# Slot tables of routing: two of each group's seven blocks multiplied by VectorE instead of ScalarE

## What is computed

```
gate_scores = einsum('bsd,ed->bse', x, Wg) + bg
topk_scores, topk_idx = top_k(gate_scores, 2)
topk_probs = softmax(topk_scores, axis=-1)
combine = sum(topk_probs[..., None] * one_hot(topk_idx, 8), axis=-2)
for e in range(8):
    h = relu(einsum('bsd,hd->bsh', x, W1[e]) + b1[e])
    y = einsum('bsh,dh->bsd', h, W2[e]) + b2[e]
    out = out + combine[..., e:e + 1] * y
```

## Time and profile before

| | us |
|---|---|
| median of three runs | 2040.22 |
| lowest and highest of them | 2038.3, 2041.55 |
| the profiled execution, its own time | 2043.48 |
| its span in the profile | 2041.8 |

### The profile page before, as it was taken

One profiled execution on the slowest core, in us unless ns is written; L12 is line 12 of the kernel. 1 busy time (PEld: TensorE's weight loads), 2 busy tenths in 40 slices (PEclk: granted clock), 3 DMA queues, 4 the chain that ended last, 5 costly groups with the idle time before them and its releaser, 6 DMA issues. The chain is left out here.

```text
span 2041.8 us, 50410 instructions
## 1 busy us (share of the span) xinstructions
PE 1662.7 (81%) x15119; PEld 1287.6 (63%) x15119; DVE 1579.0 (77%) x3370; ACT 1379.6 (68%) x3988; POOL 1247.3 (61%) x1226
## 2 busy tenths in 40 slices
PE   5777668888888788898886666562799999999998
PEld 3455557666666577777764344342677777777776
DVE  8899859898888899989998989887355555555554
ACT  7565458788887778888878878575455555555554
POOL 4357757777777777777777777650344444444443
PEclk7899979999999999999999999855899999999999
DMA  6122355555554544444433346461344444444442
GB/s 223 44 70 80 110 167 157 158 157 159 153 160 151 158 139 124 124 124 121 122 106 101 102 154 185 130 206 26 78 72 73 73 74 71 72 74 71 74 71 43
DMA packets 197501, 232.75 MB, mean 114 GB/s; under 512 B 89207, under 2 KB 154657, under 8 KB 197123
## 3 DMA queue, kind: packets, MB, share of 16 engines
q0 software_dynamic: 62816, 134.68, 25.8%
q1 hardware_dynamic: 128070, 88.47, 15.4%
q10 hardware_dynamic: 6364, 6.40, 0.9%
HBM read 172.28 MB, written 44.36 MB: 106 GB/s over the span
## 5 line engine op out<-in xcount | busy, mean ns | idle before, releaser
L1011 POOL DMA_INDIRECT misc<-z_d,consts x814 | 784.6, 964 | 265.0 <-issue 160.6
L1261 DVE SCALAR_TENSOR_TENSOR acc<-ps,consts,acc 128x512 f32 x814 | 609.2, 748 | 79.3 <-PE ps L1363 60.7
L1034 ACT ACTIVATE misc<-misc 128x256 f16<-128x256 f16 x872 | 391.2, 498 | 74.5 <-DVE misc L1128 69.0
L1891 ACT ACTIVATE misc<-ps,misc 128x128 f32<-128x128 f32 x840 | 240.2, 368 | 276.1 <-PE ps L1851 166.9
L1361 PE MATMUL ps<-misc 128*128 128x256 f16 x1088 | 298.1, 274 | 110.7 <-ACT misc L1034 35.6
L1939 POOL DMA_INDIRECT out<-misc,pos x105 | 166.4, 1585 | 295.5 <-ACT misc L1960 244.7
L1849 PE MATMUL ps<-acc,big 128*128 128x128 f16 x1680 | 328.3, 220 | 14.9 <-DMA acc<-acc 10.0
L1851 PE MATMUL ps<-acc,big 128*128 128x128 f16 x1680 | 330.0, 220 | 0.0
L1850 PE MATMUL ps<-acc,big 128*128 128x128 f16 x1680 | 327.9, 220 | 0.0
L1870 PE MATMUL ps<-big,rec 128*128 x840 | 320.5, 382 | 0.1
L1363 PE MATMUL ps<-misc 128*128 128x256 f16 x1088 | 298.8, 275 | 0.0
(11 more groups left out here) (348 smaller groups left out, 3657.8 us busy)
## 6 DMA issues: line engine op xcount, KB each, us to landing
big<-in_w2T SPq DMA_DIRECT2D x60, 256.0 KB, 2.7
misc<-z_d,consts POOLq DMA_INDIRECT x814
big<-xT_d SPq DMA_DIRECT2D x98, 128.0 KB
big<-in_w1T SPq DMA_DIRECT2D x32, 256.0 KB, 2.8
tok_d<-misc SPq DMA_DIRECT2D x50, 132.0 KB, 1.8
xT_d<-misc SPq DMA_DIRECT2D x49, 128.0 KB
z_d<-misc SPq DMA_DIRECT2D x49, 128.0 KB, 1.7
acc<-in_x SPq DMA_DIRECT2D x6, 896.0 KB
```

Source lines behind the costliest of these rows:

```text
L1011: e.indirect_dma_start(out=rows[n % RB], out_offset=None, in_=c.z_d, in_offset=bass.IndirectOffsetOnAxis(ap=idx[u][:, k:k + 1], axis=0)).t ...
L1034: e.activation(hot[n % HG][:, half, :], same[n % OG], ACT.Copy, scale=near[n // UG % 3][:, t % UG, 1 + half:2 + half]).then_inc(s_hot, 1)
L1261: e.scalar_tensor_tensor(out=rows_of, in0=out_ps[tile % BG], scalar=c.gain, in1=rows_of, op0=ALU.mult, op1=ALU.add).then_inc(s_add, 1)
L1891: l = e.activation(hidden[:, m, :], h_ps[u][:, m, :], ACT.Relu, bias=b1x[u][:, m:m + 1])
```

## The change

VectorE multiplies the last two blocks of each group (`NA` = 5 and 6) in two instructions of 2 x 105 elements, one for each of the two choices. Here `near_no` is a second tensor input, one value repeated over 105 elements. ScalarE does the blocks 0 to 4 alone. The new instructions stand in `hots`, between `hot_tile` and `hot_row`, and wait for `hot_tile` and for `s_used`; `hot_row` no longer stands directly behind that wait. `group(g)` waits for a new semaphore `s_rest` as well.

```diff
+    s_rest = S("near_rest")
+    NA = 5
+    of_blocks = lambda a, lo, hi: a.rearrange("p (k n) m -> p k n m", k=TOP)[:, :, lo:hi, :]
...
                 e.tensor_tensor(hot_tile[g % 2], row_no[:, 0:MT, :], tiled(both16[0][:, g, :], MT), ALU.is_equal).then_inc(s_tiles, 1)
+                e.wait_ge(s_tiles, g + 1)
                 if g >= 2:
                     e.wait_ge(s_used, g - 1)
+                for k in range(TOP):
+                    l = e.tensor_tensor(of_blocks(pieces[g % 2][:, :, 0, :], NA, GB)[:, k],
+                                        of_blocks(hot_tile[g % 2].rearrange("p m c -> p c m"), NA, GB)[:, k],
+                                        near_no[:, g * GB + NA:g * GB + GB].rearrange("p (n a) -> p n a", a=1).to_broadcast([P, GB - NA, MT]),
+                                        ALU.mult)
+                l.then_inc(s_rest, 1)
                 e.tensor_tensor(hot_row[g % 2], row_no, tiled(both16[1][:, g, :], P), ALU.is_equal).then_inc(s_rows, 1)
 
             def group(g):
                 e.wait_ge(s_near, g + 1)
+                e.wait_ge(s_rest, g + 1)
                 e.tensor_scalar(pieces[g % 2][:, :, 1, :], pieces[g % 2][:, :, 0, :], 0.0, float(g), ALU.is_gt,
                                 ALU.mult).then_inc(s_group, 1)
...
-                halves = lambda a, n: a.rearrange("p (k n) m -> p k n m", k=TOP)[:, :, n, :]
-                for n in range(GB):
+                halves = lambda a, n: of_blocks(a, n, n + 1)[:, :, 0, :]
+                for n in range(NA):
                     l = e.activation(halves(pieces[g % 2][:, :, 0, :], n),
```

## The result

| | before | changed |
|---|---|---|
| median, us (14 runs each) | 2041.11 | 2045.01 |
| lowest to highest | 2038.3 to 2043.81 | 2042.93 to 2049.44 |
| the profiled execution, its own time | 2043.48 | 2042.93 |
| its span | 2041.8 | 2041.2 |
| the block: first `hot_tile` to first gather | 35.32 | 39.71 |

The ratio of the times is 1.0022 with a 95% interval of 1.0015 to 1.003: slower by 3.1 to 6.1 us, 4.5 in the middle; the two medians stand 3.90 apart. 2044.8 had been predicted. The two profiled executions seem to say the opposite, since the changed one is 0.6 us shorter. The next view, busy time by stretch (PE, PEld, DVE, ACT, POOL, clock, DMA share, GB/s), divides each span into what lies ahead of the block, the block, and what lies behind it; first the kernel before.

What follows compares the result with a forecast made beforehand. The prediction took TensorE and VectorE waiting on each other in the slot-table block as the bound, not ScalarE. Its terms -0.55, +4.6 and +0.58 summed to +4.6 us, 2044.8 us against the median of 2040.22; range 2041.5 to 2047.7.

Steps and rivals of the forecast that it cites:

- The ring of TensorE and VectorE: Slot-table block: matmuls need line 1759, queued behind hot_row, which waits for the matmuls before; closes in 4.38 us per group.
- The rival that went by ScalarE's busy share: In the block, ScalarE was the bound, so its 14 removed instructions give back 8.2 us, 2032.0; chance 0.03.
- The product, 538 ns taken: Each new VectorE multiplication of 210 elements: 1.81 ns per element on 158 ns fixed, adding 0.46 us to VectorE's row.
- the low end: New VectorE multiplication priced as contiguous, 377 ns for 210 elements; as a rival, sum +2.4, 2042.6 us, chance 0.19.
- The dearer 2.50: Rival for the new multiplications' small-step read: 2.5 ns per element, 683 ns each, +6.6, 2046.8 us; chance 0.10.
- Term 2: Groups 1 to 5: two products between TensorE's release and hot_row lengthen each turn by 0.92 us; +4.6 us.
- Term 3: Block's beginning: four products and two waits for hot_tile ahead of the first line 1759, less 1.40 to give; +0.58 us.
- Term 1: Block's end: relieved ScalarE is ready earlier, so TensorE's 0.55 us wait before the last group goes; -0.55 us.
- The sum: Whole block: 14 s - 1.81 = +4.6 us, s being 0.46 us per product; against the median of 2040.22, 2044.8.
- The cover: Behind the block: nothing hides it, so what it gains or loses passes on whole.
- The verdict on an edge: Whole kernel: 4.6 us, 0.23%, against about 0.2%, 4.1 us, that can be told from no change; slower 0.55, same 0.39.
- The clock rival: Inside the block, TensorE's clock rises from the second group, saving 1.3 us per turn; -1.9, 2038.3 us; chance 0.03.

Runs made afterwards that it cites:

- e2_relief: Changed kernel without the two products and their waits, GpSimd writing zeros once instead, ScalarE doing five blocks; 0.9982 of the kernel before, block 33.09 us.
- e3_swap_before: Kernel before, ScalarE doing all seven blocks, with the next group's hot_row moved behind the group's number; 0.9997 of the kernel before, block 34.63 us.
- e6_contig: Changed kernel plus two products per group reading hot_tile contiguously, written to an unused place; one run, block 43.71 us.
- e4_swap_after: Changed kernel with the next group's products and hot_row moved behind the group's number; 0.9961 of the kernel before, block 28.89 us.
- e8_swap_scalar: Changed kernel with products in per-partition scalar form, they and hot_row moved behind the group's number; 0.9969 of the kernel before, block 27.57 us.
- e1_behind: Changed kernel with only the two products moved behind the group's number; 0.9994 of the kernel before, block 33.58 us.
- e5_double: Changed kernel plus two more products of the same pattern per group, ahead of the true ones, written to an unused place; 1.0056 of the kernel before.
- e7_scalar: Changed kernel with products as one instruction per block using a per-partition scalar, same place; 1.0013 of the kernel before, block 37.59 us.

## Why the prediction was right, step by step

- **The bound.** The ring of TensorE and VectorE is shown by e2_relief, where ScalarE's relief left 4.38 us untouched, and by e3_swap_before, where only the order was changed and the bound moved to ScalarE. The rival that went by ScalarE's busy share fails on e2_relief. It was wrong about this kernel; with the ring open ScalarE is the bound, and its relief gains 5.7 us.
- **The product, 538 ns taken, 526 measured.** VectorE's own line 1691 (513) was as near as ScalarE's row with the same pattern. e6_contig confirms the low end, 375 ns. What the step adds was not ScalarE's 0.99 ns per element but 151 / 210 = 0.72; 538 came near because ScalarE's contiguous rate, 0.816, is below VectorE's 1.045 by about as much, which is luck. By the 1.73 ns per element of the Trainium skill ("Vector Engine (DVE) Microarchitecture Reference", section 5.2) an estimate would be 521; measured are (526 - 158) / 210 = 1.75, so the trace agrees with that figure within 2%. The dearer 2.50, which the section gives for both sources or the output alone, was not met by one input with a step of 28 bytes.
- **Term 2, +4.6.** Five rings of 5.31 against 4.38 make 4.65; from the first group's matmuls to the sixth's it was 26.58 against 21.88, +4.70. Two deviations cancel in it. The two products lengthen VectorE's row by 0.87 and not by 0.92, but the first of them starts 2.75 us behind the start of the matmuls, where `hot_row` had started 2.68 behind it. These 0.07 us per ring the prediction had counted as nothing; the wait ahead of the product has a second semaphore beside it, but no run tests whether that is the reason.
- **Term 3, +0.58.** From the first `hot_tile` to the first matmul 6.35 against 5.79: +0.56. Here too the products take less than said, 1.75 instead of 1.84, and the waits for `hot_tile` more: the first product starts 0.96 behind its start, so about 0.11 are lost each time and not 0.07.
- **Term 1, -0.55: too small.** From the sixth group's matmuls to line 1767 it was 5.42 us before and is 4.55 now, -0.87. The gap of 0.55 is gone as said. But groups that follow each other without a gap also stand closer, 2.43 apart rather than 2.64, and the last takes 2.08 instead of 2.19, at a granted clock of 0.69 instead of 0.64.
- **The sum** in the block: 0.56 + 4.70 - 0.87 = 4.39, predicted 4.6. That 2045.01 lies only 0.2 us from the 2044.8 predicted is luck: the kernel before had a median of 2041.11 in these runs instead of 2040.22, and the medians stand 3.90 apart. The cover was as said: none, since the stretch behind the block is unchanged.
- **The verdict on an edge** is not decided by 14 runs each. The 4.5 us of the ratio lie above the 4.1 taken as the limit of what can be told, the 3.90 between the medians below it, and the interval of 3.1 to 6.1 takes in both. Only the sign is clear.
- **The clock rival** did not happen in the changed kernel, 0.50 up to the last group. In two of the three open rings, e4_swap_after and e8_swap_scalar, the clock did rise.

## What to carry to other kernels

Before relieving the busiest engine of a loop, follow one turn of it from release to release: an engine with a busy share of 96% can still be the one that waits, and the bound can be a ring of two engines that are busy only half the time or a little more. In such a ring it is the place in the queue that costs, not the work: what stands between a wait and the instruction that another engine needs is paid in full, and behind that instruction it is free as long as its engine has idle time there (1.09 us were left in e1_behind). When an edit with a plausible purpose loses time, try it with the ring opened before giving it up; here the block lost 4.4 us by it with the ring closed and gained 5.7 with the ring open.

## What the runs showed of the hardware

The granted clock rose in the middle of two open rings and fell again. Busy time by stretch of e4_swap_after, its first two groups, the next two, and the last three:

```profile
1611.16:1617.60 6.44, 5.11 (x28) 4.25 (x29) 6.44 (x11) 5.80 (x11) 0.00 (x0) 0.58 0.00 0
1617.60:1624.00 6.40, 2.96 (x28) 2.61 (x28) 6.40 (x11) 5.88 (x11) 0.00 (x0) 0.95 0.01 1
1624.00:1633.20 9.20, 7.92 (x42) 6.41 (x42) 5.57 (x10) 5.43 (x10) 0.00 (x0) 0.50 0.00 0
```

At 0.95, almost the full 2.4 GHz, 14 matmuls take 1.48 us instead of 2.64; TensorE then waits longer, and the next stretch is back at 0.50, 1.2 GHz. In e8_swap_scalar the third group alone took 1.48 us, at 0.96. In e3_swap_before, whose ring is open too but bound by ScalarE, TensorE works 2.64 of 3.99 us and the granted clock was 0.50 in all seven groups. In the closed rings, where TensorE works 2.64 of 4.38 to 6.18 us, the granted clock was 0.50 throughout the middle. With VectorE as the bound the faster matmuls bring e4_swap_after little: its groups were 3.2 us apart in all three stretches.

At the end of the block the clock differs from run to run, and with it the time of the last 14 matmuls. Here are those of e4_swap_after and of e8_swap_scalar.

```profile
1630.48 2.64 PE L1811 MATMUL ps<-misc,acc 128*128 128x210 f16 x14 [0.60 <-DVE misc L1772]
```

```profile
1420.53 1.64 PE L1810 MATMUL ps<-misc,acc 128*128 128x210 f16 x14 [0.50 <-DVE misc L1771]
```

The granted clock of these stretches was 0.50 and 0.88. In the other runs it was 0.64 (before, 2.19 us), 0.69 (changed, 2.08), 0.82 (e1_behind, 1.76), 0.79 (e2_relief, 1.83), 0.50 (e3_swap_before, 2.64), 0.58 (e5_double, 2.46), 0.70 (e6_contig, 2.05) and 0.90 (e7_scalar, 1.62). Each kernel has one trace, so how much this differs between executions of the same kernel is not shown.

VectorE's instructions also grew a little in the open ring: the products' median is 552 to 562 ns in e4_swap_after and 536 to 538 in e1_behind, against 526 in the changed kernel. In these two runs more engines work at the same time, but no run tests whether that is the reason.
